# The three bf16 parts of the channel gate and of the spatial statistics, read from the upper halves of f32 words

## The chip, the cores and the metric

One core of one Trainium2 chip runs the whole program. The metric is the device time of one execution in microseconds (us). The engines are TensorE (PE in the rows; PEld is its weight load), VectorE (DVE), ScalarE (ACT), GpSimd (POOL) and SyncE (SP), each with its own instruction stream, joined by semaphores.

## The reference

The input is `(16, 512, 24, 8)` in f32: 16 images of 192 tokens with 512 channels.

```python
def _L0_conv_ref(x, fc1_w, fc2_w, sa_w):        # of the channel-normalised x
    avg = jnp.mean(x, axis=(2, 3)); mx = jnp.max(x, axis=(2, 3))
    def mlp(v):
        return jax.nn.relu(v @ fc1_w.T) @ fc2_w.T
    ca = jax.nn.sigmoid(mlp(avg) + mlp(mx))     # channel gate, (16, 512)
    x = x * ca[:, :, None, None]
    s = jnp.concatenate([mean over channels, max over channels])
    s = 7x7 convolution of s with sa_w, padding 3
    return x * jax.nn.sigmoid(s)                # token gate

x = x + _L0_conv_ref(_ln_c(x), fc1_w, fc2_w, sa_w)
t = _to_tokens(x)
t = t + _L0_ffn_ref(_ln_t(t), w1, w2)           # 512 -> 2048 -> 512, gelu between,
x = _from_tokens(t, x)                          # both inputs rounded to 8 bits, weights to -1, 0, 1
```

## The kernel before

The images are taken two at a time: a pair has 384 tokens, three tiles of 128 tokens (partitions) by 512 channels, and there are eight pairs, 0 to 7. Each engine has its own program, written out by hand in its order; nothing reorders it. Pairs 0 and 1 and the weights are prepared by a long prologue. After it, `body(pair)` runs once for each pair c: it finishes the feed-forward part of pair c, does the normalisation and the first half of the feed-forward of pair c+1 (`nxt`), the attention part of pair c+2 (`att`), and loads and transposes pair c+3 (`fresh`). So the attention part of pair 2 lies in the first body and that of pair 7 in the sixth, which has no fresh pair; the last two bodies have no attention part.

The attention part of one pair goes as follows. TensorE transposes the normalised tile `v` (L1074), VectorE and ScalarE pool it over the tokens, two small products (L1084, L1090) and a tanh give the gate, and VectorE's `split_gate` turns it into `ca` and splits it into three bf16 parts. TensorE transposes the parts (`turn_ca`, L1096), ScalarE copies them to `caT`, and `spread_ca` (L1104) sums the three parts back while it spreads the gate over the tokens. VectorE multiplies (`scale_channels`, L782) into `pv` and leaves the channel maximum in `ch_stat[..., 1]`; ScalarE's `sum_channels` leaves the mean in `ch_stat[..., 0]`. Then `split_stats` splits the 2 x 3 statistics of each partition into three bf16 parts, and `conv` (L1117) does the 7x7 convolution as 42 small matmuls against band matrices, whose moving operand is the three parts, and VectorE sums what the three gave (`sum_conv`, L802).

A split is a chain on VectorE in which each step waits for the one before it (`link`): cast the f32 value to bf16 (part 0), subtract it from the value, cast the rest (part 1), subtract again (part 2).

What stands around the change, in the order of each engine in a body: on VectorE `add_attention` of tile 1 of `nxt` (t at L815, st at L817, mv at L819), `split_gate`, `centre` (cen at L827, amax at L828, lim at L831, q at L834), `hidden_max` (amax at L842), `scale_channels` of tiles 0 and 1, two `channel_stats` of the fresh pair (L744), `scale_channels` of tile 2, `aggregate` (mv at L750), `hidden_max`, `hidden_scale` (L850, q at L852), `split_stats`, `channel_stats` of the third fresh tile, `sum_conv`. On TensorE the convolution is the last thing of a body, behind the transposes of the fresh pair's third tile (L1064), and the next body begins with sixteen matmuls of `ffn_in` (L1141), `turn_res` (L1161) and `turn_v1` (L1074), which needs the three tiles `v` of the fresh pair. These come from GpSimd's `normalise1` (L444 to L446, then v at L451): tiles 0 and 1 ahead of `round_g` (w_room at L474, two instructions), tile 2 behind it.

Of the kernel before, what the change touches and what calls it, by code (L numbers as in the profile page):

```python
# [5 lines left out]
def metaformer_kernel(nc, x, fc1_w, fc2_w, sa_w, w1, w2, out):  # L6
# [11 lines left out]
    f32, f16, bf16 = mybir.dt.float32, mybir.dt.float16, mybir.dt.bfloat16  # L18
# [26 lines left out]
    with ctx:  # L45
# [72 lines left out]
        stat_r1 = sb("stat_r1", [P, NT, 2])  # L118
        stat_split = sb("stat_split", [P, NT, 2, 3], bf16)
# [4 lines left out]
        ca = sb("ca", [P, NC, 2])  # L124
        ca_r1 = sb("ca_r1", [P, NC, 2])
        ca_split = sb("ca_split", [P, NC, 2, 3], bf16)
        caT = sb("caT", [6, C], bf16)
        ch_stat = [sb(f"ch_stat{i}", [P, NT, 2]) for i in range(2)]
# [186 lines left out]
        def low_halves(ap):  # L315

            return ap.bitcast(f16).rearrange("p (c two) -> p c two", two=2)[:, :, 0]

# [195 lines left out]
        def _(act):  # L514
# [35 lines left out]
            def sum_channels(tile):  # L550
                wait(act, scaled, tile.at(1, 1))
                wait(act, stat_ready, tile.pair.at(1, -1))
                wait(act, summed, tile.at())
                copy(junk_p[:, :], pv[tile.pair.par][:, tile.s, :], summed, scale=1.0 / C,
                     accum_out=ch_stat[tile.pair.par][:, tile.s, 0:1])
# [159 lines left out]
        def _(dve):  # L715
# [51 lines left out]
            def split_gate(pair):  # L767

                wait(dve, ca_tanh_ready, pair.at(1, 1))
                wait(dve, ca_turned, pair.at(1))  # L770
                link(dve.tensor_scalar(ca[:, :, :], ca_tanh[:, :, :], 0.5, 0.5, ALU.mult, ALU.add))
                link(dve.tensor_copy(ca_split[:, :, :, 0], ca[:, :, :]))
                link(dve.tensor_tensor(ca_r1[:, :, :], ca[:, :, :], ca_split[:, :, :, 0], ALU.subtract))
                link(dve.tensor_copy(ca_split[:, :, :, 1], ca_r1[:, :, :]))
                dve.tensor_tensor(ca_split[:, :, :, 2], ca_r1[:, :, :], ca_split[:, :, :, 1],
                                  ALU.subtract).then_inc(ca_ready, 1)

            def scale_channels(tile, bank):
# [5 lines left out]
                                         op1=ALU.max, accum_out=ch_stat[tile.pair.par][:, tile.s, 1:2]  # L784
                                         ).then_inc(scaled, 1)

            def split_stats(pair):

                wait(dve, summed, pair.at(NT, NT))
                wait(dve, scaled, pair.at(NT, NT))  # L790
                wait(dve, conv_done, pair.at(1))
                st = ch_stat[pair.par][:, :, :]
                link(dve.tensor_copy(stat_split[:, :, :, 0], st))
                link(dve.tensor_tensor(stat_r1[:, :, :], st, stat_split[:, :, :, 0], ALU.subtract))
                link(dve.tensor_copy(stat_split[:, :, :, 1], stat_r1[:, :, :]))
                dve.tensor_tensor(stat_split[:, :, :, 2], stat_r1[:, :, :], stat_split[:, :, :, 1],
                                  ALU.subtract).then_inc(stat_ready, 1)
# [260 lines left out]
        def _(pe):  # L1058
# [34 lines left out]
            def turn_ca(pair):  # L1093
                wait(pe, ca_ready, pair.at(1, 1))
                for k in range(NC):
                    last = pe.transpose(caT_ps[0:6, tile_cols(k)],  # L1096
                                        ca_split[:, k, :, :].rearrange("p i j -> p (i j)"), idb[:, :])
                last.then_inc(ca_turned, 1)
# [9 lines left out]
            def conv(pair):  # L1108

                wait(pe, stat_ready, pair.at(1, 1))  # L1110
                for o in range(NT):
                    near = [i for i in range(NT) if abs(i - o) <= 1]
                    terms = [(i, ch, j) for i in near for ch in range(2) for j in range(3)]
                    for n, (i, ch, j) in enumerate(terms):
                        rows = ROWS * (o - i + 1)
                        mat = band_mid[:, j, ch] if i == o == 1 else band[:, j, ch, rows:rows + ROWS]
                        last = pe.matmul(conv_ps[:, o, :], mat.rearrange("p r w -> p (r w)"), stat_split[:, i, ch, :],  # L1117
# [246 lines left out]
```

## Time and profile before

| | |
|---|---|
| device time, median of 3 runs | 321.71 us (321.67 to 323.82) |
| device time of the profiled execution | 321.15 us |
| span of its instructions | 319.4 us |
| mean granted TensorE clock | 0.951 of full speed |
| PE busy | 275.2 us (86%) |
| DVE busy | 256.8 us (80%) |
| ACT busy | 218.0 us (68%) |
| POOL busy | 162.4 us (51%) |
| DVE instructions | 590 |

The span runs from the first to the last instruction of the profiled execution; 1.75 us of its device time lie outside it. Busy shares are averages over stages with different limits. The prologue lasts until about 80 us, the bodies fill the rest, and from pair 2 on a body repeats about every 31.6 us. In the rows, times are in us from the start of the span unless marked ns.

### The profile page before, as it was taken

How to read it: one execution, taken by the hardware profiler on the slowest of the kernel's cores; microseconds unless marked ns; L12 is line 12 of the kernel's file. 1: busy time of each engine (PE TensorE's matmuls, PEld its weight loads, DVE VectorE, ACT ScalarE, POOL GpSimd, SP SyncE). 2: the span in 40 equal slices, each digit the busy share in tenths (PEclk: the TensorE clock that was granted, in tenths of full speed). 3: DMA queues.
4: the chain of work that ended last, by engine and by line, in shares of the span. 5: the costliest groups of instructions: out<-in, count | busy, mean ns of one | idle time of the engine just before them, and what ended most of it. 6: DMA issues, size and time to landing. Idle time of an engine off the chain costs nothing.

```text
span 319.4 us, 5840 instructions
## 1 busy us (share of the span) xinstructions
PE 275.2 (86%) x1834; PEld 153.2 (48%) x1834; DVE 256.8 (80%) x590; ACT 218.0 (68%) x442; POOL 162.4 (51%) x256
## 2 busy tenths in 40 slices
PE   3557659696899999999999999989999998899974
PEld 2444534543456355535553556455535553444431
DVE  1757979979698979897989798989997988799510
ACT  2286397578666878687868786858687757577731
POOL 7404355324855385538553855475538552455410
PEclk9999775959799999999999999999999999999999
DMA  4899400002373028402941294128402631263493
GB/s 132 315 382 422 131 1 2 0 0 43 26 167 66 12 57 232 99 19 49 240 92 27 39 230 102 34 36 222 109 19 49 165 69 23 45 164 67 79 218 99
DMA packets 71078, 34.20 MB, mean 107 GB/s; under 512 B 52040, under 2 KB 68424, under 8 KB 70536
## 3 DMA queue, kind: packets, MB, share of 16 engines
q1 hardware_dynamic: 69384, 32.78, 41.0%
q10 hardware_dynamic: 1664, 1.05, 1.2%
q8 instruction: 15, 0.25, 0.3%
q14 instruction: 15, 0.12, 0.1%
HBM read 14.94 MB, written 6.29 MB: 66 GB/s over the span
## 4 chain that ended last, share of the span: by engine, by line
PE 49%; DVE 27%; issue 9%; ACT 6%; POOL 4%; DMA 3%; SPq 1%; ACTq 0%; DVEq 0%; POOLq 0%
PE ps_o L1152 17%; PE ps_h L1141 9%; PE ps_t L1141 8%; DVE amax L842 4%; PE front L1074 3%; PE small L1117 3%; DVE t L815 3%; PE front L1161 2%; ACT junk L520 2%; PE ps_t L1183 2%; DVE st L817 2%; DVE amax L828 2%; DVE w_room L885 2%; DVE pv L782 2%; PE front L1126 1%
## 5 line engine op out<-in xcount | busy, mean ns | idle before, releaser
L1152 PE MATMUL ps_o<-w2T,hq 128*128 128x512 f16 x384 | 92.7, 380 | 1.2 <-DMA hq<-w_raw 1.2
L474 POOL TENSOR_SCALAR w_room<-w_room,q 128x1024 f32<-128x1024 f32 x48 | 59.0, 1241 | 54.6 <-DVE q L852 54.6
L842 DVE TENSOR_REDUCE amax<-w_room 128x1 f32<-128x1024 f32 (+1 forms) x48 | 57.1, 1208 | 2.2 <-ACT w_room L520 2.2
L1141 PE MATMUL ps_h<-w1T,xq 128*128 128x512 f16 x208 | 55.3, 412 | 1.0 <-ACT xq L520 1.0
L1152 PEld LDWEIGHTS ps_o<-w2T,hq 128*128 128x128 f16 x384 | 35.4, 98 | 37.3 <-issue 3.6
L520 ACT ACTIVATE w_raw<-w_room 128x1024 f16<-128x1024 f16 x48 | 50.1, 1048 | 0.6 <-POOL w_room L474 0.6
L520 ACT ACTIVATE w_room<-ps_h,s 128x512 f32<-128x512 f32 x52 | 35.1, 690 | 15.4 <-PE ps_h L1141 14.3
L1141 PE MATMUL ps_t<-w1T,xq 128*128 128x512 f16 x176 | 42.6, 379 | 0.0
L520 ACT ACTIVATE w_room<-ps_t,s 128x512 f32<-128x512 f32 x44 | 30.3, 688 | 7.7 <-PE ps_t L1141 7.6
L1141 PEld LDWEIGHTS ps_h<-w1T,xq 128*128 128x128 f16 x208 | 20.2, 105 | 25.1 <-issue 6.4
L520 ACT ACTIVATE junk_m<-front 128x192 bf16<-128x192 f32 x64 | 20.5, 331 | 16.2 <-DVE pooled L757 16.2
L463 POOL TENSOR_SCALAR cen<-cen,q 128x512 f32<-128x512 f32 x24 | 16.7, 695 | 27.4 <-DVE q L834 27.4
L859 DVE SCALAR_TENSOR_TENSOR res<-ps_o,s,t 128x512 f32<-128x512 f32 x24 | 17.9, 748 | 13.1 <-PE ps_o L1152 13.1
L1141 PEld LDWEIGHTS ps_t<-w1T,xq 128*128 128x128 f16 x176 | 16.7, 98 | 20.1
L744 DVE BATCH_NORM_STATS2 st<-xt 128x6 f32<-128x512 f32 x24 | 15.7, 684 | 9.3 <-ACT xt L520 9.3
L1064 PE MATMUL front<-id,x_in 128*128 128x128 f32 x96 | 17.0, 314 | 6.8 <-DMA x_in<-in_x 5.6
L1074 PE MATMUL front<-id,v 128*128 128x128 f32 x96 | 18.1, 311 | 5.2 <-POOL v L451 2.5
L815 DVE SCALAR_TENSOR_TENSOR t<-pv,sg,xt 128x512 f32<-128x512 f32 x24 | 21.0, 876 | 0.3
L451 POOL TENSOR_SCALAR v<-xt,minus_mean,rs 128x512 f32<-128x512 f32 x24 | 20.0, 839 | 1.4
L520 ACT ACTIVATE w_room<-front 128x512 f32<-128x512 f32 x24 | 14.1, 586 | 8.8 <-PE front L1161 8.8
L757 DVE TENSOR_REDUCE pooled<-front 128x2 f32<-128x384 f32 x32 | 17.5, 548 | 2.4 <-PE front L1074 2.2
L520 ACT ACTIVATE junk_p<-pv 128x512 bf16<-128x512 f32 x24 | 15.0, 627 | 5.4 <-DVE ch_stat L782 4.6
(125 smaller groups left out, 458.3 us busy)
## 6 DMA issues: line engine op xcount, KB each, us to landing
out<-w_room SPq DMA_DIRECT2D x16, 384.0 KB, 3.3
x_in<-in_x SPq DMA_DIRECT2D x14, 384.0 KB, 5.3
w_room<-in_L_ffn_w SPq DMA_DIRECT2D x4, 1024.0 KB, 8.9
w_raw<-in_L_ffn_w SPq DMA_DIRECT2D x4, 1024.0 KB, 12.1
x_in<-in_x ACTq DMA_DIRECT2D x2, 384.0 KB, 3.7
hq<-w_raw SPq DMA_TRANSPOSE x48, 3.2
fc_raw<-in_L_conv_fc_w ACTq DMA_DIRECT2D x2, 128.0 KB, 4.1
taps_rev<-in_L_conv_sa_w SPq DMA_DIRECT2D x2, 0.2 KB
```

What stands on the lines that cost most here:

```text
L451: pool.tensor_scalar(v1[:, s, :], xt[pair.par][:, s, :], minus_mean[:, s:s + 1], rs1[:, s:s + 1], ALU.add, ALU.mult).then_inc(normed, 1)
L463: pool.tensor_scalar(c[:, :], c[:, :], q1[tile.par][:, 0:1], MAGIC, ALU.mult, ALU.add).then_inc(cen_rounded, 1)
L474: pool.tensor_scalar(part, part, q2[tile.par][:, 0:1], MAGIC, ALU.mult, ALU.add).then_inc(g_rounded, 1)
L520: act.activation(out_ap, in_ap, func, **more).then_inc(signal, 1)
L757: dve.tensor_reduce(pooled[:, k, 0:2], front[bank][:, 0:TOK].rearrange("p (i t) -> p i t", i=2), AX.X, ALU.max).then_inc(max_ready, 1)
L815: link(dve.scalar_tensor_tensor(t_tile, pv[par][:, s, :], sg[par][:, s:s + 1], xt[par][:, s, :], ALU.mult, ALU.add))
L842: chain.mark(dve.tensor_reduce(amax2[:, i:i + 1], w1_room[:, first + i * F // 2:first + (i + 1) * F // 2 + i], AX.X, ALU.max, apply_absolu ...
L859: dve.scalar_tensor_tensor(res[tile.par][:, :], ps_o[:, :], s2[tile.third][:, 0:1], t[tile.pair.par][:, tile.s, :], ALU.mult, ALU.add).the ...
L1064: last = pe.transpose(front[bank][:, tile_cols(k)], x_in[tile.pair.par][:, k, tile_cols(tile.s)], id32[:, :])
L1074: last = pe.transpose(front[bank][:, tile_cols(s)], v1[:, s, tile_cols(k)], id32[:, :])
L1141: last = pe.matmul(banks[b], xq[tile.pair.par][:, tile.s, k, :], w1T[:, k, b * 512:(b + 1) * 512], start=(k == 0), stop=(k == NC - 1))
L1152: last = pe.matmul(ps_o[:, :], hq[tile.par][:, k, :], w2T[:, k, :], start=(k == 0), stop=(k == NF - 1))
```

## The change

The casts that made parts 0 and 1 are gone from `split_gate` and `split_stats`. The f32 value is kept in slot 0 of a group of three f32 words, the first rest in slot 1, the second rest in slot 2, and where a bf16 part was read before, the upper 16 bits of the slot are read, as a bf16 view with a step of two elements. Part 0 is so the value cut off at 16 bits rather than rounded, and the rest is taken from that. The tensors `stat_r1`, `stat_split`, `ca_r1` and `ca_split` are gone; `ca` and `ch_stat` are three times as wide. The convolution now reads `ch_stat` itself, which has two buffers, by the pair's parity. The number of matmuls, of transposes and of their columns stays. The splits of the convolution's taps, once in the prologue, stay too.

```diff
-        ca = sb("ca", [P, NC, 2])
-        ca_r1 = sb("ca_r1", [P, NC, 2])
-        ca_split = sb("ca_split", [P, NC, 2, 3], bf16)
+        ca = sb("ca", [P, NC, 2, 3])
-        ch_stat = [sb(f"ch_stat{i}", [P, NT, 2]) for i in range(2)]
+        ch_stat = [sb(f"ch_stat{i}", [P, NT, 2, 3]) for i in range(2)]
...
+        def high_words(ap):
+
+            return ap.bitcast(bf16).rearrange("p (n j two) -> p n j two", j=3, two=2)[:, :, :, 1]
...
-                link(dve.tensor_scalar(ca[:, :, :], ca_tanh[:, :, :], 0.5, 0.5, ALU.mult, ALU.add))
-                link(dve.tensor_copy(ca_split[:, :, :, 0], ca[:, :, :]))
-                link(dve.tensor_tensor(ca_r1[:, :, :], ca[:, :, :], ca_split[:, :, :, 0], ALU.subtract))
-                link(dve.tensor_copy(ca_split[:, :, :, 1], ca_r1[:, :, :]))
-                dve.tensor_tensor(ca_split[:, :, :, 2], ca_r1[:, :, :], ca_split[:, :, :, 1],
-                                  ALU.subtract).then_inc(ca_ready, 1)
+                parts = ca[:, :, :, :].rearrange("p k i j -> p (k i) j")
+                heads = high_words(ca[:, :, :, :].rearrange("p k i j -> p (k i j)"))
+                link(dve.tensor_scalar(parts[:, :, 0], ca_tanh[:, :, :].rearrange("p k i -> p (k i)"), 0.5, 0.5,
+                                       ALU.mult, ALU.add))
+                link(dve.tensor_tensor(parts[:, :, 1], parts[:, :, 0], heads[:, :, 0], ALU.subtract))
+                dve.tensor_tensor(parts[:, :, 2], parts[:, :, 1], heads[:, :, 1], ALU.subtract).then_inc(ca_ready, 1)
...
-                link(dve.tensor_copy(stat_split[:, :, :, 0], st))
-                link(dve.tensor_tensor(stat_r1[:, :, :], st, stat_split[:, :, :, 0], ALU.subtract))
-                link(dve.tensor_copy(stat_split[:, :, :, 1], stat_r1[:, :, :]))
-                dve.tensor_tensor(stat_split[:, :, :, 2], stat_r1[:, :, :], stat_split[:, :, :, 1],
-                                  ALU.subtract).then_inc(stat_ready, 1)
+                link(dve.tensor_tensor(parts[:, :, 1], parts[:, :, 0], heads[:, :, 0], ALU.subtract))
+                dve.tensor_tensor(parts[:, :, 2], parts[:, :, 1], heads[:, :, 1], ALU.subtract).then_inc(stat_ready, 1)
...
-                                        ca_split[:, k, :, :].rearrange("p i j -> p (i j)"), idb[:, :])
+                                        heads[:, 2 * k:2 * k + 2, :].rearrange("p i j -> p (i j)"), idb[:, :])
...
-                        last = pe.matmul(conv_ps[:, o, :], mat.rearrange("p r w -> p (r w)"), stat_split[:, i, ch, :],
+                        last = pe.matmul(conv_ps[:, o, :], mat.rearrange("p r w -> p (r w)"), heads[:, 2 * i + ch, :],
```

VectorE's order at the gate in a body, before: `mv` and `t` are those of `add_attention`, `cen` that of `centre`.

```order
L819 BN_AGGR mv_1<-st 128x2
L771 TENSOR_SCALAR ca<-ca_tanh 128x8
L772 CAST ca_split<-ca 128x8
L773 TENSOR_TENSOR ca_r<-ca,ca_split 128x8
L774 CAST ca_split<-ca_r 128x8
L775 TENSOR_TENSOR ca_split<-ca_r,ca_split 128x8
L827 TENSOR_SCALAR cen<-t,mv_1 128x512
```

The same place now, with the line numbers of the changed kernel:

```order
L818 BN_AGGR mv_1<-st 128x2
L773 TENSOR_SCALAR ca<-ca_tanh 128x8
L775 TENSOR_TENSOR ca<-ca 128x8
L776 TENSOR_TENSOR ca<-ca 128x8
L826 TENSOR_SCALAR cen<-t,mv_1 128x512
```

Two casts have gone, and nothing else has changed its place.

VectorE's order at the statistics in a body, before: `q` is that of `hidden_scale`, for which GpSimd's w_room at L474 waits.

```order
L782 ISA ch_stat 128x1
L750 BN_AGGR mv<-st 128x2 x2
L842 TENSOR_REDUCE amax<-w_room 128x1
L850 TENSOR_SCALAR lim<-amax 128x1
L852 RECIPROCAL q_0<-lim 128x1
L793 CAST stat_split<-ch_stat 128x6
L794 TENSOR_TENSOR stat_r<-ch_stat,stat_split 128x6
L795 CAST stat_split<-stat_r 128x6
L796 TENSOR_TENSOR stat_split<-stat_r,stat_split 128x6
L744 BN_STATS st<-xt 128x6
```

And now:

```order
L782 ISA ch_stat 128x1
L750 BN_AGGR mv<-st 128x2 x2
L841 TENSOR_REDUCE amax<-w_room 128x1
L849 TENSOR_SCALAR lim<-amax 128x1
L851 RECIPROCAL q_0<-lim 128x1
L795 TENSOR_TENSOR ch_stat<-ch_stat 128x6
L796 TENSOR_TENSOR ch_stat<-ch_stat 128x6
L744 BN_STATS st<-xt 128x6
```

Here too two casts have gone from between `q` and the statistics of the fresh tile; the first subtraction now follows `q` directly.

## Rows read from the trace of the kernel before

**Rows 1.** Windows from t (L815) to t, two bodies: us, busy of PE, PEld, DVE, ACT, POOL, clock, DMA

```profile
132.96:164.61 31.65, 30.57 (x211) 16.67 (x211) 28.31 (x70) 23.86 (x52) 18.57 (x31) 1.00 0.43 101
196.21:228.77 32.56, 30.22 (x211) 16.72 (x211) 29.57 (x69) 23.81 (x52) 18.54 (x31) 1.00 0.45 98
```

**Rows 2.** Timeline at the statistics of pair 4: start, duration, engine, line, operation, idle before

```profile
174.79 1.55 POOL L451 TENSOR_SCALAR v<-xt,minus_mean,rs 128x512 f32<-128x512 f32 x2
174.92 0.17 DVE L793 CAST stat_split<-ch_stat 128x6 bf16<-128x6 f32 x1
175.13 0.45 DVE L794 TENSOR_TENSOR stat_r<-ch_stat,stat_split 128x6 f32<-128x6 f32 x1
175.61 0.18 DVE L795 CAST stat_split<-stat_r 128x6 bf16<-128x6 f32 x1
...
175.73 0.60 PE L1064 MATMUL front<-id,x_in 128*128 128x128 f32 x4
175.82 0.54 DVE L796 TENSOR_TENSOR stat_split<-stat_r,stat_split 128x6 bf16<-128x6 f32 x1
...
176.42 0.60 PE L1117 MATMUL small<-stat_split,band 128*128 128x3 bf16 x18
```

**Rows 3.** Timeline in the gate stage of the same pair

```profile
166.46 0.21 DVE L772 CAST ca_split<-ca 128x8 bf16<-128x8 f32 x1
...
166.91 0.18 DVE L774 CAST ca_split<-ca_r 128x8 bf16<-128x8 f32 x1
...
169.02 1.21 DVE L842 TENSOR_REDUCE amax<-w_room 128x1 f32<-128x1024 f32 x1
...
169.74 0.60 PE L1104 MATMUL front<-caT,img_pick 6*128 6x512 bf16 x2
...
170.17 0.69 DVE L782 CUSTOM_DVE_ANT_0 pv<-v,front 128x512 f32<-128x512 f32 x1
```

**Rows 4.** Timeline in the body after pair 4's statistics, and in the one after pair 5's

```profile
180.44 1.00 POOL L451 TENSOR_SCALAR v<-xt,minus_mean,rs 128x512 f32<-128x512 f32 x1
180.95 0.60 PE L1161 MATMUL front<-id,res 128*128 128x128 f32 x4
...
181.50 0.55 PE L1074 MATMUL front<-id,v 128*128 128x128 f32 x3
...
213.61 0.60 PE L1161 MATMUL front<-id,res 128*128 128x128 f32 x4
...
214.05 0.49 PE L1074 MATMUL front<-id,v 128*128 128x128 f32 x3
```

**Rows 5.** Chain that ended last, same body: two groups of ps_o matmuls with a transpose between

```profile
184.10 0.86 PE ps_o L1152 x4
185.36 0.86 PE ps_o L1152 x4
```

**Rows 6.** Timeline at the statistics of pair 5

```profile
206.88 0.32 DVE L793 CAST stat_split<-ch_stat 128x6 bf16<-128x6 f32 x1 [0.30 <-issue]
...
207.22 0.20 DVE L794 TENSOR_TENSOR stat_r<-ch_stat,stat_split 128x6 f32<-128x6 f32 x1
...
207.99 1.05 DVE L796 TENSOR_TENSOR stat_split<-stat_r,stat_split 128x6 bf16<-128x6 f32 x1
```

**Rows 7.** Timeline from the gate to the convolution of pair 7

```profile
264.82 0.60 PE L1104 MATMUL front<-caT,img_pick 6*128 6x512 bf16 x2
...
265.01 1.21 DVE L842 TENSOR_REDUCE amax<-w_room 128x1 f32<-128x1024 f32 x1
...
266.14 0.68 DVE L782 CUSTOM_DVE_ANT_0 pv<-v,front 128x512 f32<-128x512 f32 x1
...
272.66 0.60 PE L1117 MATMUL small<-stat_split,band 128*128 128x3 bf16 x18 [0.81 <-DVE stat_split L796]
```

**Rows 8.** Timeline at the convolution of pair 0 and behind that of pair 1

```profile
35.59 0.62 PE L1117 MATMUL small<-stat_split,band 128*128 128x3 bf16 x18 [2.74 <-DVE stat_split L796]
...
79.89 2.22 POOL L474 TENSOR_SCALAR w_room<-w_room,q 128x1024 f32<-128x1024 f32 x2 [2.33 <-DVE q L852]
...
86.60 0.55 PE L1074 MATMUL front<-id,v 128*128 128x128 f32 x3 [1.09 <-POOL v L451]
```

More of the change, by code:

```diff
@@ L117, in metaformer_kernel @@
         pooled = sb("pooled", [P, NC, 4])
-        stat_r1 = sb("stat_r1", [P, NT, 2])
-        stat_split = sb("stat_split", [P, NT, 2, 3], bf16)
         conv_sum = sb("conv_sum", [P, NT])
@@ L554, in sum_channels @@
                 copy(junk_p[:, :], pv[tile.pair.par][:, tile.s, :], summed, scale=1.0 / C,
-                     accum_out=ch_stat[tile.pair.par][:, tile.s, 0:1])
+                     accum_out=ch_stat[tile.pair.par][:, tile.s, 0, 0:1])
             def gate_tokens(pair):
@@ L783, in scale_channels @@
                                          in1=front[bank][:, :], scale=1.0, scalar=-3.0e38, op0=ALU.mult,
-                                         op1=ALU.max, accum_out=ch_stat[tile.pair.par][:, tile.s, 1:2]
+                                         op1=ALU.max, accum_out=ch_stat[tile.pair.par][:, tile.s, 1, 0:1]
                                          ).then_inc(scaled, 1)
@@ L791, in split_stats @@
                 wait(dve, conv_done, pair.at(1))
-                st = ch_stat[pair.par][:, :, :]
-                link(dve.tensor_copy(stat_split[:, :, :, 0], st))
-                link(dve.tensor_tensor(stat_r1[:, :, :], st, stat_split[:, :, :, 0], ALU.subtract))
-                link(dve.tensor_copy(stat_split[:, :, :, 1], stat_r1[:, :, :]))
-                dve.tensor_tensor(stat_split[:, :, :, 2], stat_r1[:, :, :], stat_split[:, :, :, 1],
-                                  ALU.subtract).then_inc(stat_ready, 1)
+                flat = ch_stat[pair.par][:, :, :, :]
+                parts = flat.rearrange("p s c j -> p (s c) j")
+                heads = high_words(flat.rearrange("p s c j -> p (s c j)"))
+                link(dve.tensor_tensor(parts[:, :, 1], parts[:, :, 0], heads[:, :, 0], ALU.subtract))
+                dve.tensor_tensor(parts[:, :, 2], parts[:, :, 1], heads[:, :, 1], ALU.subtract).then_inc(stat_ready, 1)
             def sum_conv(pair):
@@ L1094, in turn_ca @@
                 wait(pe, ca_ready, pair.at(1, 1))
+                heads = high_words(ca[:, :, :, :].rearrange("p k i j -> p (k i j)"))
                 for k in range(NC):
                     last = pe.transpose(caT_ps[0:6, tile_cols(k)],
-                                        ca_split[:, k, :, :].rearrange("p i j -> p (i j)"), idb[:, :])
+                                        heads[:, 2 * k:2 * k + 2, :].rearrange("p i j -> p (i j)"), idb[:, :])
                 last.then_inc(ca_turned, 1)
@@ L1110, in conv @@
                 wait(pe, stat_ready, pair.at(1, 1))
+                heads = high_words(ch_stat[pair.par][:, :, :, :].rearrange("p s c j -> p (s c j)"))
                 for o in range(NT):
```

## The prediction

> **What bounds the kernel now.** I read the windows first, cut at the start of the same t (L815) in every body, because they say how regular the bodies are. One with a convolution at its end takes 31.65 us and PE is busy for 30.57 of it [rows 1], so no body can win more than about a microsecond unless something is wrong in it. Something is: the window that holds pair 5's statistics takes 32.56 us with the same work [rows 1]. Next comes the chain of waits around each convolution, since both edits stand on VectorE ahead of it, and then the timeline, to see who is late by how much once the edit is made. Three things are to be seen there.
>
> First, at pair 4's statistics the two casts take 0.17 and 0.18 us and delay nobody, but the subtractions take 0.45 and 0.54 us for six elements, where one takes 0.20 in [rows 6]. The first ends at 175.58, the second at 176.36; the two GpSimd instructions v, started at 174.79 and together 1.55 us long, end at about 175.57 and 176.34 [rows 2]. A subtraction that meets a running GpSimd instruction ends when that one does. The convolution starts at 176.42, right behind the second.
>
> Second, TensorE had nearly as much to do: the four transposes ahead of the convolution start at 175.73 and take 0.60 with the tail of the last one, which a following matmul overlaps, so that it was ready at about 176.2 [rows 2]. The convolution waits for the statistics for some 0.2 us only.
>
> Third, the next body has a wait of its own behind it: turn_v1 starts at 181.50, right after GpSimd's third v (180.44 plus 1.00), 0.55 us behind L1161; in the body after pair 5 it is 0.44 (213.61 to 214.05), so that 0.11 is waiting [rows 4]. That v comes from the fresh pair through the bn_stats (L744), GpSimd's v and w_room, not through the convolution.
>
> **The change, part by part.** The gate: a cast goes at L772 (0.21 us and about 0.04 to the next start) and one at L774 (0.18 and 0.03) [rows 3], 0.46 us of VectorE. In a body this hardly counts. pv (L782) starts at 170.17, when amax (L842, 169.02 plus 1.21) ends; but the spread that it reads started only at 169.74, 0.43 earlier, and the first of its two matmuls has landed after about 0.4 (0.60 for both, less 0.21 for one) [rows 3, 5]. VectorE comes 0.46 earlier and then waits for TensorE: 0.02 us are left. That holds for pairs 2 to 6, five bodies, 0.1 us together. The cover is TensorE's and ScalarE's way to the spread; without it each would give 0.46.
>
> Pair 7 is the other case: no fresh pair is transposed in its body, the spread is out at 264.82 plus 0.60, and pv starts at 266.14 only because amax runs from 265.01 for 1.21 us [rows 7]. Here the whole 0.46 us pass on, through pv, ScalarE's sums and its copy that frees TensorE's bank.
>
> The statistics: each cast costs 0.21 us from start to start (174.92 to 175.13) [rows 2], 0.42 for the two, if nothing of GpSimd's is in the way. In pairs 2, 3, 4 and 6 v is in the way. The first subtraction will start where the first cast did, 0.13 us behind v, and end with it at 175.58; the second starts at about 175.61, where the second cast started and passed in 0.18 us, right at the start of the next v [rows 2]. Does a subtraction pass there too? At pair 5 one started at 207.22, just behind a cast that had waited, and took 0.20 us [rows 6]. I take it that it passes; the bounds are 0.20 (passing) and 0.54 (waiting for the second v, as now). Passing, the statistics are ready at 175.8, TensorE at 176.2, and the convolution starts about 0.2 us earlier.
>
> What of that is left? Not all, because turn_v1 already waits for v. But behind it the ps_o groups at 184.10 (four matmuls, 0.86 us) and 185.36 leave 1.26 us for 0.86 of work and four transposes of 128 columns, at the same rate 0.22 [rows 5]; the rest, some 0.18, is TensorE waiting for its bank, which ScalarE frees in a row of work that began with the first gelu after the convolution. This row moves with the convolution. I take 0.15 us a body, between 0 and 0.2, five times: 0.75 us.
>
> Pair 5: the first cast starts after an idle 0.30 us and takes 0.32, the last subtraction 1.05, waiting for a whole w_room as well [rows 6]. Its window is 0.91 us longer than the others [rows 1]. With two steps for four, both subtractions are through before w_room begins. I take the 0.91 back in full.
>
> Pair 7: the convolution waits 0.81 us [rows 7], a little more without the tail of the matmul ahead: 0.9. In the next body there is no attention part and no v, so nothing else holds TensorE. With the gate's 0.46 that is 1.36 us.
>
> The prologue: at pair 0 TensorE idles 2.74 us before the convolution and waits for the last subtraction [rows 8], with no GpSimd work beside; the weights' transposes stand behind it, and VectorE's next work shifts as well, so 0.42 us. Its gate lies under ScalarE's squares: nothing. At pair 1 the convolution is covered by transposes, but q (L852) stands behind the split on VectorE, and w_room at 79.89, idle until that q, then the three v and turn_v1 at 86.60, which waits 1.09 us for them, all follow from it [rows 8]: another 0.42. The gate of pair 1 is covered by weight transposes.
>
> What is added: the same matmuls read their three columns with a step of two. No row shows a moving operand read so. From below nothing can be won, as the load beside it takes its time anyway; I take 0 for it, and for the bound above see the slower rival. The wider ch_stat costs nothing that a row shows.
>
> The sum: 0.10 + 0.75 + 0.91 + 1.36 + 0.42 + 0.42 = 3.96, say 4.0 us. The profiled execution took 321.15 us, 0.56 less than the median of 321.71; its successor should take 317.2, and the median 317.7. A change of under 1% (3.2 us) is what a measurement of this kernel can't tell from none.
>
> **The rivals.** *The second subtraction doesn't pass.* It waits for the second v in pairs 2 to 6, the convolution starts where it does now, and the 0.75 goes: gain 3.2, 318.5 us. For it: each subtraction that began 0.2 us into a GpSimd instruction waited [rows 2]; against: the 0.20 us at 207.22 [rows 6]. The Trainium skill (SBUF — State Buffer, Who interferes with whom) would have it so: whichever of the two starts first holds the shared pair for its whole instruction, and v starts first. By that rule the sum is this rival's; the 0.20 us at 207.22 speaks against a rule without a margin. Chance 0.2.
>
> *The prologue and pair 5 don't pay.* The 0.42 at pairs 0 and 1 have to pass through 45 us of work in which some other wait, or a TensorE clock that rises at another moment, can absorb them, and pair 5's stall may be chance that comes again in another pair. Then 1.36 and about 0.85 of the bodies are left, 2.2 us: 319.5. Chance 0.2.
>
> *The casts had kept the subtractions out of GpSimd's way.* The first subtraction now asks 0.13 us into v, where only a cast has passed. If it wins the pair only after the second v, the second waits for one w_room, as at pair 5, and a body costs the 0.91 more that its window shows [rows 1, 6]. In pairs 2, 3, 4 and 6 that is 3.6 us, pair 5 stays as it is, pair 7 gives less: with 0.84 from the prologue and 0.46 from pair 7 the end is 324 us. It decides from two waits in a row; the one wait of a subtraction at the start of v, ending with it, speaks against. A step in the moving operand would act the same way from 12 ns a matmul (42 in each of eight convolutions, 4.0 us). Chance 0.05.
>
> *More than forecast.* If the runs behind the median hold two such stalls each, as the 0.56 between them and the profiled one hints, both go: 316.8. Chance 0.1.
>
> **How the numbers follow.** The forecast, gain 3.3 to 4.6, has 0.45. The range takes in the forecast's bounds, the first two rivals and the upside: 316.6 to 320.0. Faster by over 1% (under 318.5): the forecast and the upside, half of the first rival, and little of the second: 0.66. Slower by over 1%: 0.02. The rest, 0.32, is within 1%.
>
> **What would show it.** In the new profile: two DVE rows of TENSOR_TENSOR at each split and no CAST. The second subtraction at 0.2 us in pairs 2 to 6, and no idle PE before their convolutions. pv in a body waiting for the spread, about 0.4 us of new idle on VectorE. All windows at 31.4 to 31.5 us and none at 32.5; pair 7's convolution 1.4 us nearer to its t. Wrong it would be if a subtraction in these pairs took over 1 us, if the 42 matmuls took longer than now, or if the windows stayed at 31.65 although the convolution starts earlier.

## The result, and the profile after

The changed kernel takes **317.42 us** (median of 4 runs, 317.06 to 318.03). The kernel before, run beside it, takes 322.49 (4 runs, 321.67 to 323.82). The ratio is 0.9844, with a 95% interval of 0.981 to 0.9879: 1.6% faster. The profiled execution took 317.06 us with a span of 315.2, against 321.15 and 319.4 before: 4.1 us less, where the medians differ by 5.1.

The page after: its first part, the granted clock in 40 slices, the start of the chain.

```profile
PE 272.2 (86%) x1834; PEld 154.7 (49%) x1834; DVE 247.3 (78%) x558; ACT 218.0 (69%) x442; POOL 161.4 (51%) x256
...
PEclk9755758879699999999999999999999999999998
...
PE 52%; DVE 15%; POOL 13%; issue 8%; ACT 7%; DMA 3%; SPq 1%; ACTq 0%; POOLq 0%; DVEq 0%
```

The windows from t (now L814) to t, columns as in [rows 1]; the last one runs from pair 7's t to the end. This t is the third of a body, that of the last tile of `nxt` (tile 2, not tile 1 as the order further up has it), and the gate of the body's attention pair is split right behind it:

```profile
131.52:163.06 31.54, 30.37 (x211) 16.76 (x211) 27.30 (x65) 23.84 (x52) 18.39 (x31) 1.00 0.43 101
...
194.60:226.18 31.58, 30.37 (x211) 16.76 (x211) 27.30 (x65) 23.84 (x52) 18.38 (x31) 1.00 0.47 101
...
257.73:315.20 57.47, 49.79 (x292) 24.23 (x291) 34.87 (x73) 34.59 (x53) 22.46 (x34) 0.98 0.42 97
```

All five bodies lie between 31.53 and 31.58, and the long one of [rows 1] is gone. The saving has three places, all against the profiled execution of before: the first window begins 1.32 us earlier (99.99 for 101.31), the five bodies take 1.55 less together (157.74 for 159.29), and the stretch from pair 7's t to the end 1.36 less (57.44 for 58.80). Together these are the 4.2 us by which the spans differ. (A last window ends at the span rounded to 0.1 us; the times from pair 7's t to the end in the text go to the end of the last instruction.)

The statistics of pair 4, in the timeline:

```profile
173.25 1.53 POOL L451 TENSOR_SCALAR v<-xt,minus_mean,rs 128x512 f32<-128x512 f32 x2
...
173.37 0.17 DVE L795 TENSOR_TENSOR ch_stat<-ch_stat 128x6 f32<-128x6 f32 x1
173.58 0.46 DVE L796 TENSOR_TENSOR ch_stat<-ch_stat 128x6 f32<-128x6 f32 x1
...
174.19 0.60 PE L1063 MATMUL front<-id,x_in 128*128 128x128 f32 x4
...
174.62 0.60 PE L1118 MATMUL small<-ch_stat,band 128*128 128x3 bf16 x18
```

This answers to [rows 2], and it is the opposite order of what was forecast. The **first** subtraction, 0.12 us into v, passes in 0.17; the **second**, 0.33 into the same v, takes 0.46 and ends at 174.04, when the first of the two v does (half of the 1.53 is 0.77). The statistics are ready before TensorE's four transposes even start (174.19), and it begins the convolution 0.43 behind them, as soon as it can. From t to the convolution it is 11.56 us for 11.81 before: the forecast 0.2 and a little more. What the next body makes of it (before, [rows 4]):

```profile
177.12 0.75 DVE L814 SCALAR_TENSOR_TENSOR t<-pv,sg,xt 128x512 f32<-128x512 f32 x1
...
177.30 0.62 POOL L444 TENSOR_SCALAR ve<-mv 128x1 f32<-128x1 f32 x1
...
178.84 1.00 POOL L451 TENSOR_SCALAR v<-xt,minus_mean,rs 128x512 f32<-128x512 f32 x1
...
179.15 0.60 PE L1162 MATMUL front<-id,res 128*128 128x128 f32 x4
...
179.90 0.55 PE L1073 MATMUL front<-id,v 128*128 128x128 f32 x3
```

turn_v1 (L1073) is now 0.75 us behind L1162, where it was 0.55 and, unhindered, 0.44. TensorE is earlier, the third v is not by as much, and the waiting has grown from 0.11 to 0.31. GpSimd is held by VectorE on the way: L444 takes 0.62 beside t (0.19 when alone), v 1.00 beside cen (0.77 alone). It was held in the same way before (0.62 and 1.00), so its row is nearly as long as it was: from the start of the first v to the end of the third 6.59 us, for 6.65. GpSimd's share of the chain rises to 13%, from 4% before.

Further on in the same body, the transposes of cen and the next ones of v, first before, then after, and a row of VectorE after:

```profile
184.98 0.38 PE L1126 MATMUL front<-id,cen 128*128 128x128 f16 x4
...
186.09 0.52 PE L1074 MATMUL front<-id,v 128*128 128x128 f32 x3
```

```profile
183.20 0.39 PE L1127 MATMUL front<-id,cen 128*128 128x128 f16 x4
...
184.48 0.52 PE L1073 MATMUL front<-id,v 128*128 128x128 f32 x3
```

```profile
180.86 0.21 DVE L830 TENSOR_SCALAR lim<-amax,rs 128x1 f32<-128x1 f32 x1 [0.77 <-POOL rs L439]
```

Counted from the body's t (164.61 and 163.06), the changed kernel is ahead by 0.25 us at the convolution and at L1162, by 0.05 at turn_v1, by 0.23 at the transposes of cen, where a wait of TensorE for its bank has gone, and by 0.06 at the next transposes of v. These wait for their bank, which ScalarE frees behind VectorE's pooling; VectorE's steps ahead of the pooling wait for GpSimd's rs behind the third v (0.77 us in both kernels), and from lim (L830) to those transposes it takes 3.62 us, for 3.63 before (182.46 to 186.09). So the convolution gains 0.25 and the row from GpSimd's v takes all but 0.06 of it back, in two places.

The gate of the same pair and the gate to the convolution of pair 7 ([rows 3], [rows 7]):

```profile
168.20 0.60 PE L1104 MATMUL front<-caT,img_pick 6*128 6x512 bf16 x2
168.62 0.69 DVE L782 CUSTOM_DVE_ANT_0 pv<-v,front 128x512 f32<-128x512 f32 x1 [0.38 <-PE front L1104]
...
261.71 1.21 DVE L841 TENSOR_REDUCE amax<-w_room 128x1 f32<-128x1024 f32 x1
261.94 0.60 PE L1104 MATMUL front<-caT,img_pick 6*128 6x512 bf16 x2
...
262.83 0.68 DVE L782 CUSTOM_DVE_ANT_0 pv<-v,front 128x512 f32<-128x512 f32 x1
...
266.90 0.17 DVE L795 TENSOR_TENSOR ch_stat<-ch_stat 128x6 f32<-128x6 f32 x1
267.11 0.17 DVE L796 TENSOR_TENSOR ch_stat<-ch_stat 128x6 f32<-128x6 f32 x1
...
268.38 0.60 PE L1118 MATMUL small<-ch_stat,band 128*128 128x3 bf16 x18
```

In pair 4 pv waits 0.38 for the spread: the cover that was named. In pair 7 pv still starts when amax ends, and the convolution starts 10.65 us behind its t, 12.06 before: 1.41 earlier, with no wait left in front of it. The split itself is shorter by much more than the two casts took: in the kernel before its second cast, 0.26 us into a w_room, took 0.91 us, and the last subtraction, 0.09 us into the next w_room, 1.05, so that the four steps took 2.41 us. Now the second subtraction, 0.06 us into the first w_room, passes, and the two take 0.38.

The prologue ([rows 8]), and the matmuls of the convolution (shortest, median and longest in ns):

```profile
35.14 0.60 PE L1118 MATMUL small<-ch_stat,band 128*128 128x3 bf16 x18 [1.79 <-DVE ch_stat L796]
...
78.41 2.21 POOL L474 TENSOR_SCALAR w_room<-w_room,q 128x1024 f32<-128x1024 f32 x2 [1.92 <-DVE q L851]
...
L1118 PE MATMUL small<-ch_stat,band x288: 164/165/213, 35.1 to 269.4; 128*128 128x3 bf16 x144
```

Both waits of [rows 8] are shorter, and the step of two in the moving operand costs nothing: a median of 165 ns a matmul, 164 before.

### The profile page after: what moved, and what is told of

The parts are those of the page before. It is cut to its first block, busy times and chain, and to the rows that moved or that the text cites. A ratio compares the mean times of both kernels' runs of the same rounds, so it can differ in the third digit from the quotient of the medians.

```text
span 315.2 us, 5808 instructions
## 1 busy us (share of the span) xinstructions
PE 272.2 (86%) x1834; PEld 154.7 (49%) x1834; DVE 247.3 (78%) x558; ACT 218.0 (69%) x442; POOL 161.4 (51%) x256
## 3 DMA queue, kind: packets, MB, share of 16 engines
q10 hardware_dynamic: 1664, 1.05, 1.2%
## 4 chain that ended last, share of the span: by engine, by line
PE 52%; DVE 15%; POOL 13%; issue 8%; ACT 7%; DMA 3%; SPq 1%; ACTq 0%; POOLq 0%; DVEq 0%
PE ps_o L1153 17%; PE ps_h L1142 9%; PE ps_t L1142 9%; POOL v L451 5%; PE front L1073 4%; POOL w_room L474 3%; PE front L1063 3%; PE ps_t L1184 2%; POOL rs L445 2%; DVE pv L782 2%; ACT junk L520 2%; PE small L1089 2%; DVE w_room L884 2%; DVE t L814 2%; PE front L1162 2%
## 5 line engine op out<-in xcount | busy, mean ns | idle before, releaser
L474 POOL TENSOR_SCALAR w_room<-w_room,q 128x1024 f32<-128x1024 f32 x48 | 59.3, 1247 | 54.3 <-DVE q L851 54.3
L1142 PE MATMUL ps_h<-w1T,xq 128*128 128x512 f16 x208 | 52.3, 394 | 1.1 <-ACT xq L520 0.8
L1142 PE MATMUL ps_t<-w1T,xq 128*128 128x512 f16 x176 | 43.3, 384 | 0.0
L1142 PEld LDWEIGHTS ps_h<-w1T,xq 128*128 128x128 f16 x208 | 19.2, 100 | 23.2 <-issue 2.4
L1073 PE MATMUL front<-id,v 128*128 128x128 f32 x96 | 18.1, 311 | 5.5 <-POOL v L451 2.1
L814 DVE SCALAR_TENSOR_TENSOR t<-pv,sg,xt 128x512 f32<-128x512 f32 x24 | 21.6, 899 | 0.3
L444 POOL TENSOR_SCALAR ve<-mv 128x2 f32<-128x2 f32 (+2 forms) x13 | 5.0, 388 | 27.8 <-DVE mv L750 27.3
```

The lines of the kernel that those rows point to most:

```text
L474: pool.tensor_scalar(part, part, q2[tile.par][:, 0:1], MAGIC, ALU.mult, ALU.add).then_inc(g_rounded, 1)
L814: link(dve.scalar_tensor_tensor(t_tile, pv[par][:, s, :], sg[par][:, s:s + 1], xt[par][:, s, :], ALU.mult, ALU.add))
L1073: last = pe.transpose(front[bank][:, tile_cols(s)], v1[:, s, tile_cols(k)], id32[:, :])
L1142: last = pe.matmul(banks[b], xq[tile.pair.par][:, tile.s, k, :], w1T[:, k, b * 512:(b + 1) * 512], start=(k == 0), stop=(k == NC - 1))
```

## The experiments

The first six kernels hold both ways of making the parts, chosen by the number of the pair. The sites read as follows, for the statistics (the gate likewise), and each kernel changes one line.

```diff
+        NEW_GATE, NEW_STAT = [0, 1, 2, 3, 4, 5, 6, 7], []
 ...
+                if pair.c not in NEW_STAT:
+                    st = ch_stat[pair.par][:, :, :, 0]
+                    link(dve.tensor_copy(stat_split[:, :, :, 0], st))
 ...
+                    return
 ...
+                                         heads[:, 2 * i + ch, :] if pair.c in NEW_STAT else stat_split[:, i, ch, :],
```

Ratios are to the kernel before on the same chip, with 95% intervals.

**The gate alone** (the line above).

> Only the gate is split the new way, the statistics the old way in all pairs. Theory (the gate is covered by TensorE's way to the spread in every body but pair 7's): 0.46 us at pair 7, 0.1 in pairs 2 to 6 together, nothing in the prologue, so 0.5 to 0.6 us less, ratio 0.998. Rival (the gate pays wherever VectorE carries the chain): 0.46 in each of six bodies, 2.8 us, ratio 0.991. The subtractions of the statistics should wait for GpSimd as in the kernel before (0.45 and 0.54 us), and a window of about 32.5 us may come up in any of pairs 2 to 6.

Measured: 320.11 us, ratio 0.994 (0.9919 to 0.9961): a larger saving than the theory's 0.998 and a smaller one than the 0.991 of its rival. The windows below say where it comes from.

**The statistics alone.**

```diff
-        NEW_GATE, NEW_STAT = [0, 1, 2, 3, 4, 5, 6, 7], []
+        NEW_GATE, NEW_STAT = [], [0, 1, 2, 3, 4, 5, 6, 7]
```

> Only the statistics are split the new way, the gate the old way. Theory: 0.84 us in the prologue, 0.1 in each of the bodies of pairs 2 to 6, 0.9 at pair 7, and no window of 32.5 us: 2.3 us, and 0.9 more for each such window that the kernel before has, ratio 0.990 to 0.993; pv should start right after amax again in the bodies. Rival (the gate is what pays): under 1 us, ratio 0.997 or more.

Measured: 318.68 us, ratio 0.9905 (0.9882 to 0.9928). Windows from t to t, of the kernel with the gate alone first, then of the one with the statistics alone:

```profile
133.38:164.97 31.59, 30.48 (x211) 16.68 (x211) 28.24 (x68) 23.85 (x52) 18.65 (x31) 1.00 0.43 100
...
259.74:318.20 58.46, 49.95 (x292) 24.15 (x291) 36.80 (x75) 34.60 (x53) 22.46 (x34) 1.00 0.43 95
```

```profile
163.34:194.91 31.57, 30.37 (x211) 16.76 (x211) 27.62 (x68) 23.87 (x52) 18.48 (x31) 1.00 0.47 101
...
258.13:315.90 57.77, 49.79 (x292) 24.23 (x291) 35.24 (x75) 34.62 (x53) 22.58 (x34) 1.00 0.43 96
```

In the bodies neither edit alone shows much: one window of 31.54 and four of 31.59 with the gate alone, 31.57 to 31.62 and one of 31.75 with the statistics alone, where the kernel before has 31.59 in the later executions below. So the gate does not pay 0.46 in every body, as its rival had it. At the end the gate gives 0.30 (58.50 us) and the statistics 1.00 (57.80), together nearly the 1.36 of both. Both kernels have lost the 32.5 window, though one of them still has all the old casts in its statistics: the first sign that pair 5's stall isn't the casts' price.

**Pairs 0 and 1 alone, and pairs 2 to 7 alone.**

```diff
+        NEW_GATE, NEW_STAT = [0, 1], [0, 1]
```

> Both splits are new in pairs 0 and 1 alone. Theory: 0.42 us at each statistics, so the first t of the first body 0.84 us earlier than in the kernel before, ratio 0.997. Rival (the 1.3 us that the prologue of the changed kernel is shorter come from the edit, through a TensorE clock that rises earlier): 1.3 us, ratio 0.996, with the same clock pattern as in the changed kernel. Second rival: absorbed, 1.000.

```diff
+        NEW_GATE, NEW_STAT = [2, 3, 4, 5, 6, 7], [2, 3, 4, 5, 6, 7]
```

> Both splits are new in pairs 2 to 7 alone. Theory: windows of 31.54 us in place of 31.65, none of 32.5, and 1.33 us at pair 7: 1.9 us, and 0.9 more for each long window of the kernel before, ratio 0.991 to 0.994. Rival (most of the measured 5 us comes from the prologue): under 1 us.

Measured: 319.48 us, ratio 0.9927 (0.9905 to 0.9948), and 318.12 us, ratio 0.9888 (0.9863 to 0.9913). The savings add up to 1.85%, where the whole change has 1.56%. The intervals are too wide to tell these apart, but the profiles show that both kernels have lost the stall of pair 5, so that it counts twice. In the first of them every body is the old one, and yet its window at pair 5 is 31.51. (Its first window is 31.94, because the t that opens it takes 1.17 us, 0.79 in the kernel with pair 7 alone.)

The first of them was to come to its first body 0.84 us earlier. In its profile the first window begins 1.46 earlier (99.85 for 101.31), with a clock pattern near the changed kernel's, which is what the rival said. One execution can't decide this: in the second kernel, whose prologue is the old one, it begins 0.33 earlier as well (100.98). The prologues of all profiled executions are compared further down.

**Old statistics in pairs 2 to 6, all else new.**

```diff
+        NEW_GATE, NEW_STAT = [0, 1, 2, 3, 4, 5, 6, 7], [0, 1, 7]
```

> The gate is new everywhere, the statistics are new in pairs 0, 1 and 7 and old in pairs 2 to 6. Theory (the third v, not the convolution, holds the next body): windows of 31.54 to 31.60 us, so 0.2 us more than the changed kernel, and 0.9 for a long window if one comes up; ratio to the kernel before 0.985 to 0.988. Rival (the prediction's 0.15 us a body from an earlier convolution): windows of 31.7, 0.75 us more than the changed kernel.

Measured: 317.95 us, ratio 0.9863 (0.9833 to 0.9894), which the interval can't tell from the 0.9844 of the whole change. Its windows are 31.65, 31.66 and three of 31.60, against 31.53 to 31.58: at most 0.07 us a body for the statistics in pairs 2 to 6, 0.37 together, where 0.75 was forecast, and not the 31.7 of the rival.

Old and new windows both come in two sizes 0.06 apart from one body to the next, so that this difference is partly chance. The two parts of a window say it better. From t to the convolution it is 11.81 or 11.82 us with old statistics and 11.55 to 11.57 with new ones, with few exceptions in all fourteen profiled executions; from the convolution to the next t, outside the stall of pair 5 and the body behind it, 19.77 to 19.84 with old ones and 19.98 to 20.05 with new ones, where GpSimd's order is the same. Of the 0.25 us about 0.2 is lost behind the convolution: 0.05 us a body is left, some 0.25 for the five.

**Pair 7 alone.**

```diff
+        NEW_GATE, NEW_STAT = [7], [7]
```

> Both splits are new in pair 7 alone. Theory: from the t of pair 7's body to the end 57.5 us where the kernel before takes 58.8, 1.3 us less, ratio 0.996; the windows ahead of it as in the kernel before, a long one by chance. Rival (part of it is lost later, behind the transfers of the last tiles): 58.0 or more.

Measured: 319.75 us, ratio 0.9919 (0.9892 to 0.9945). The stretch from pair 7's t to the end takes 57.40 us in the profile, 1.40 less than before: the forecast 1.36 in one place. The long window is back, 32.57 at pair 5. But 0.8% of the median is 2.6 us, more than the 1.4 that the profile shows; the executions of the kernel before, below, offer a reason.

**The v wait for the statistics.** In this kernel and the next two the base is the changed kernel. GpSimd starts the first v of a body only when the statistics are ready.

```diff
+                if pair.c >= 3 and tiles[0] == 0:
+                    wait(pool, stat_ready, pair.at(1))
```

> The changed kernel, and GpSimd's first v of a body also waits until the statistics are split. Theory (a subtraction that meets a running v waits for it, and turn_v1 waits for the third v): both subtractions take 0.17 us, the first v starts about 0.3 us later, turn_v1 too, and each of the five windows grows by about 0.3 us: 1.5 us more than the changed kernel. Rival (v has slack): windows stay at 31.55. Second rival (the 0.46 us have another cause than v): the second subtraction still takes 0.46.

Measured: 320.76 us, ratio 0.9939 (0.9917 to 0.9961). Timeline at pair 4's statistics, and a window:

```profile
176.07 0.17 DVE L797 TENSOR_TENSOR ch_stat<-ch_stat 128x6 f32<-128x6 f32 x1
176.27 0.17 DVE L798 TENSOR_TENSOR ch_stat<-ch_stat 128x6 f32<-128x6 f32 x1
```

```profile
165.76:197.96 32.20, 30.36 (x211) 16.80 (x211) 27.57 (x65) 23.97 (x52) 18.36 (x31) 1.00 0.42 99
```

With no v beside them both subtractions take 0.17, in every pair: the 0.46 is the running v, and nothing in the operation. The v starts 0.69 us behind q, where it started 0.02 ahead of it: it is 0.71 us later, not the 0.3 that was expected, and the bodies take 0.64 more. Nine tenths of a delay of GpSimd's row reach the end of the body. The bodies hang on that row, from v to turn_v1 and on to the next transposes, and not on the convolution, which starts 11.56 us behind t here too.

**The third v earlier.** It goes ahead of the rounding of g.

```diff
                         normalise1(pair.plus(3), 0, 1)
+                        normalise1(pair.plus(3), 2)
 ...
-                if turn:
-                    normalise1(pair.plus(3), 2)
```

> The changed kernel with GpSimd's third v ahead of w_room (round_g) in its order. Theory: turn_v1 no longer waits (0.3 us a body), w_room comes about 1.5 us later, which ScalarE's packing can bear; windows of 31.3 us, 1 us less than the changed kernel, ratio to the kernel before 0.981. Rival (the later w_room and the rsqrt behind it delay the next q and TensorE's transposes): windows of 31.6 or more.

Measured: 327.56 us, ratio 1.013 (1.0088 to 1.0171): the rival held. Window, and timeline behind the third v:

```profile
169.16:202.27 33.11, 30.33 (x211) 16.68 (x211) 28.11 (x66) 23.97 (x52) 18.39 (x31) 1.00 0.41 97
```

```profile
182.55 0.19 POOL L444 TENSOR_SCALAR ve<-mv 128x1 f32<-128x1 f32 x1 [1.67 <-DVE mv L749]
...
184.88 2.38 POOL L474 TENSOR_SCALAR w_room<-w_room,q 128x1024 f32<-128x1024 f32 x2
184.96 1.32 DVE L825 TENSOR_SCALAR cen<-t,mv 128x512 f32<-128x512 f32 x1
```

GpSimd now stands 1.67 us waiting for the fresh pair's moments, with w_room queued behind. That w_room then runs under cen, which takes 1.32 us instead of 0.51. Four windows take 33.10 to 33.16, the first 34.74: there TensorE's granted clock also fell to half for some 3 us. Here the v may not be ahead of work that is ready sooner.

**GpSimd's small step s behind the third v.** `between` is the third v; s (L478) comes after it.

```diff
-            def round_g(tile):
+            def round_g(tile, between=None):
 ...
+                if between:
+                    between()
```

> The changed kernel with GpSimd's small step s (L478, 0.27 us) behind the third v instead of ahead of it. Theory: its ve (L444) then starts before VectorE's t and is not held by it for 0.4 us, and the third v comes 0.3 to 0.6 us earlier; turn_v1 starts right behind turn_res, and each of the five windows is about 0.3 us shorter (31.25 us): 1.5 us less than the changed kernel, ratio to the kernel before 0.980. Rival (VectorE's cen then meets v and the next q and transposes come later): windows of 31.55 or more.

Measured: 317.95 us, ratio 0.9849 (0.982 to 0.9877), not to be told from the changed kernel. Timeline at the third v, and a window:

```profile
178.57 0.95 POOL L445 TENSOR_TENSOR rs<-ve,half_pow 128x1 f32<-128x1 f32 x1
...
179.80 0.76 POOL L451 TENSOR_SCALAR v<-xt,minus_mean,rs 128x512 f32<-128x512 f32 x1
...
180.40 0.60 PE L1163 MATMUL front<-id,res 128*128 128x128 f32 x4
...
180.84 0.49 PE L1074 MATMUL front<-id,v 128*128 128x128 f32 x3
```

```profile
164.30:195.73 31.43, 30.24 (x211) 16.68 (x211) 27.52 (x65) 23.87 (x52) 18.26 (x31) 1.00 0.47 102
```

turn_v1 is again 0.44 behind the transposes ahead of it, and the bodies take 31.42 to 31.46: 0.12 less than in the changed kernel, where 0.3 was expected. So the third v is part of what keeps the bodies at 31.54; that much of the statistics' gain could be had back. The median doesn't show these 0.6 us: the profile's first window begins at 101.46, 1.47 later than in the changed kernel's, with another clock pattern in the prologue. The wait for VectorE moves from L444 to the next step (0.95 for 0.55).

**The kernel before, three more executions.** They ask whether the long window stays at pair 5, and why medians and profiled execution differ.

> The kernel before, looked at again. Theory (a long window is a matter of a few hundredths of a microsecond between the first cast and v): some of its five windows take 32.5 us in some looks and 31.6 in others; four windows of five or more at 31.6. Rival (it is fixed): exactly pair 5's window takes 32.5 us each time.

> The kernel before, looked at once more, for the same question: whether the long window of 32.5 us moves from look to look, or is pair 5's each time.

> The kernel before, looked at a third time, for the same question: whether the long window of 32.5 us moves from look to look, or is pair 5's each time.

Measured: 322.58, 324.37 and 322.04 us. The long window is pair 5's in all three: 32.55, 34.23 and 32.56, with 31.59 or 31.60 in the three ahead of it and 31.82 or 31.83 behind. My theory that it moves from one execution to the next has fallen. The first of them, from pair 5's t, in windows and in the timeline:

```profile
195.89:228.44 32.55, 30.22 (x211) 16.72 (x211) 29.56 (x69) 23.81 (x52) 18.50 (x31) 1.00 0.45 98
...
260.27:320.80 60.53, 51.57 (x292) 24.56 (x291) 37.14 (x77) 34.63 (x53) 22.41 (x34) 0.97 0.40 92
```

```profile
206.07 1.51 POOL L451 TENSOR_SCALAR v<-xt,minus_mean,rs 128x512 f32<-128x512 f32 x2
206.55 0.31 DVE L793 CAST stat_split<-ch_stat 128x6 bf16<-128x6 f32 x1 [0.30 <-issue]
...
207.12 0.50 DVE L795 CAST stat_split<-stat_r 128x6 bf16<-128x6 f32 x1
...
207.66 1.05 DVE L796 TENSOR_TENSOR stat_split<-stat_r,stat_split 128x6 bf16<-128x6 f32 x1
```

In every pair from 2 to 6 the v starts 0.02 us ahead of q, and the first step of the split 0.12 or 0.13 behind the v. Only here it comes 0.48 behind it: VectorE idles 0.30 with nothing to wait for ("issue"). Late, the cast no longer passes; the steps behind it meet the second v and a w_room. The idle 0.29 or 0.30 stands at the same place of VectorE's own list in each of five executions whose list is before's up to there (these three, the profiled one, pair 7 alone): in front of recorded operation 406, which is entry 576 of VectorE's records if its waits on semaphores are counted too. The kernel with new pairs 0 and 1 has eight operations fewer ahead. Its timeline at pair 5:

```profile
208.07 0.17 DVE L823 TENSOR_REDUCE conv_sum<-small 128x3 f32<-128x9 f32 x1
208.50 0.18 DVE L756 BATCH_NORM_AGGREGATE mv<-st 128x2 f32<-128x6 f32 x1 [0.27 <-issue]
```

The idle 0.27 is there again, six operations behind the first cast of the split, where it costs little. By operations this is the 404th and not the 406th; counted with the waits it is entry 576 once more. In the eight other executions entry 576 is itself a wait, recorded while a VectorE instruction of 0.7 us runs (the gate or the statistics alone, pairs 2 to 7 alone, the old statistics in pairs 2 to 6) or two short steps behind a wait of 0.42 to 1.51 us for GpSimd (the changed kernel and the three built on it), and no such idle shows. So the stall follows the length of VectorE's list up to there, waits included, and it hurts where it falls among short steps. Six executions agree with that; no run moved it on purpose, and what happens in VectorE at that entry stays open.

The last stretch is the other finding: 60.57, 60.36 and 60.24 us, against 58.80 in the profiled execution. In windows of 2 us, of the first of the three:

```profile
272.00:274.00 2.00, 1.67 (x44) 1.34 (x45) 0.69 (x3) 0.15 (x1) 0.49 (x2) 0.82 0.68 131
274.00:276.00 2.00, 2.00 (x6) 0.68 (x5) 1.93 (x4) 0.74 (x2) 0.00 (x0) 0.50 0.03 8
```

TensorE's granted clock falls to half, the 1.2 GHz level, right behind pair 7's convolution and stays there for about 3 us. The same eight matmuls in its timeline, and in that of the profiled kernel before, where the clock stays up:

```profile
273.41 3.49 PE L1141 MATMUL ps_h<-w1T,xq 128*128 128x512 f16 x8
```

```profile
273.74 1.89 PE L1141 MATMUL ps_h<-w1T,xq 128*128 128x512 f16 x8
```

Ahead of that TensorE had been lightly used for some microseconds (1.25 us of 2 from 270 on) and had then waited 0.81 for the statistics. In the second of the three the clock also fell behind pair 5's stall, to 0.53 in 210 to 212; that is its 34.23. With old statistics in pair 7 it fell in three of six profiled executions; with new ones, where TensorE does not wait there, in none of eight. This is a count, not a test of its own: the three others (the profiled kernel before, the gate alone, pairs 0 and 1 alone) have the same wait of 0.81 behind the same work, and their clock stays up. What tells the two groups apart is not shown.

## Why the prediction was right, point by point

**The time.** 317.7 was forecast, 317.42 measured. The forecast gain was 4.0 us against the profiled execution, and the two profiled executions differ by 4.1. The terms fared less evenly than the sum, and that it came out so close is in part luck, as the prologue below shows.

**The gate in pairs 2 to 6, 0.1 us**: right that it is next to nothing. pv waits 0.38 for the spread, and the gate alone has windows of 31.59, as the kernel before has in its later executions; 0.02 a body is too little to be read.

**The statistics in pairs 2, 3, 4 and 6 and in pair 5, 0.75 us together**: this step failed, in its mechanism and its size. That the first subtraction waits and the second passes ("I take it that it passes") was the wrong way round: the first passes and the second waits for the first v. What tells them apart at pair 4 is how far behind the start of a v an operation comes, and [rows 2] held it already: counted from the start of the v that ran, 0.13 passed, 0.34 waited, about 0.04 passed, about 0.25 waited, cast or subtraction alike. The row that I leaned on, 207.22 with 0.20, is another of some 0.07 by that count. It isn't the whole rule: the last subtraction of pair 5 in [rows 6] starts 0.09 us into a w_room and waits for all of it, as does the one of pair 7 in each execution with old statistics there. What makes 0.07 pass and 0.09 wait, and 0.13 pass behind another v, is open. The wait now ends 0.7 us before the second v would, so that the rival (it waits for the second v, and the convolution starts as before) has the mechanism of a wait and not its consequence. The convolution did come 0.25 us earlier. What was over-sized is what the next body keeps. I took 0.15 from the wait for ScalarE's bank further on. That wait did go (from 0.05 ahead to 0.23 ahead at the transposes of cen), but turn_v1 waits for the third v, which I had named and then left out of the price, and the next transposes of v wait behind the same v by way of VectorE and ScalarE. Old against new in pairs 2 to 6 is 0.05 to 0.07 a body, 0.25 to 0.37 in all, for a term of 0.75.

The Trainium skill (SBUF — State Buffer, Who interferes with whom) says that a VectorE instruction with two SBUF inputs contends with a GpSimd instruction that reads SBUF, and that the one that issues first holds the shared ports for its whole instruction. The second subtraction agrees (0.46, ending with v), and both at 0.17 when v waits. The first does not: 0.12 or 0.13 us behind v's start it passes, in every pair from 2 to 6 of every kernel that has it there.

**Pair 5, 0.91 us in full**: right and a little small. The body behind it was slow too (31.83 for 31.59), so that some 1.2 us came back. That "with two steps for four, both subtractions are through" is the wrong reason: kernels with the old four steps lost the stall as well. As far as the executions show, it goes because the list of VectorE's instructions is another.

**Pair 7, 0.9 and 0.46, 1.36 together**: right. 1.36 in the changed kernel, 1.40 with pair 7 alone, and apart 1.00 for the statistics and 0.30 for the gate. The convolution starts 0.98 and 0.44 earlier with either alone, as the two terms said.

**The prologue, 0.84 us**: right at its two sources, and not shown where it counts. For pair 1: from the third t to the fourth, the first of the first body, it is 9.79 to 9.93 us in the seven profiled executions with old statistics there, 9.37 to 9.52 in the seven with new ones. Each range is two groups, by when TensorE's clock falls near the fourth t: 9.79 or 9.80 against 9.37 or 9.38 where it falls at 77.2 to 78.7, 9.92 or 9.93 against 9.51 or 9.52 where it falls at 78.9 to 80.7. That is 0.42 and 0.41 for the forecast 0.42. For pair 0: the first convolution and the first t come 0.40 us earlier in the mean of seven against seven (t at 39.68 for 40.08). But the first window begins at 99.85 to 101.64 with the new prologue and at 100.91 to 101.84 with the old one, 0.44 apart in the mean: in the first clock group 1.1 earlier, in the second 0.1. The groups are read off the profiles; no run sets the clock. So the 1.32 of the two profiled executions is more than the edit can be given credit for; the one of before is of the second group, the one of after of the first. The rival (a clock that rises at another moment absorbs it) has these four of the seven new prologues for it.

**Slower (the casts kept the subtractions out of the way; 12 ns a matmul)**: didn't occur. No subtraction of the statistics over 0.47, and 165 ns for 164.

**More than forecast**: the medians did differ by 5.1 us and not 4.0, but not by two stalls of pair 5. The kernel before loses 1.4 to 1.8 us behind pair 7 in the three executions in which TensorE's clock falls there, and in one of them as much again at pair 5. The profiled execution that I worked from had neither. This would also account for pair 7 alone gaining 2.6 in the median and 1.4 in the profile; the other executions behind the medians have no profile that could show it.

The sum against the profile thus came out by errors that cancel: some 0.5 too much for the bodies, and 0.3 at pair 5 and 0.5 in the prologue too little, the last of these by the clock.

## What to carry to other kernels

Removing small instructions from an engine pays where another engine waits for the last of them and nothing else is late: here 1.4 us for four instructions in pair 7, against 0.05 to 0.07 a body for the same edit where GpSimd's third v was next in line. Before pricing an earlier start, follow the next body to whoever waits there already, and price that wait as if it took the whole gain. And look at several executions of the kernel before: a half-clock stretch that the profiled one happens not to show is part of what its median costs, and of what removing a wait can win.

## What was unexpected of the hardware

- A VectorE instruction of 6 elements a partition with two inputs from SBUF passes beside GpSimd's first v when it starts 0.12 or 0.13 us behind it (0.17 us), and waits until that one ends when it starts 0.33 behind it (0.46 us). Beside a w_room one passed 0.06 behind its start (0.17 us) and one waited 0.09 behind it (1.05 us).
- VectorE idles 0.27 to 0.30 us, waiting for nothing that the profile shows, in front of entry 576 of its records (operations and waits), in six executions of three kernels; among short instructions that cost the kernel before 1.2 us.
- A wait of 0.81 us of TensorE behind a lightly used stretch was followed in three of six executions by some 3 us at half the granted clock, in which eight matmuls took 3.49, 3.34 and 3.22 us for 1.89.
- The moving operand of a matmul, three bf16 columns read with a step of two, costs the same as without the step (a median of 165 and 164 ns).
